# Phase ends without GpSimd's drain, and three reorderings in the middle phase of a macaron block

## The chip, the cores and the metric

The kernel runs on one core of a Trainium2 chip. Its engines are PE (TensorE, matmuls), ACT (ScalarE), DVE (VectorE), POOL (GpSimd, which here also issues the indirect DMAs) and SP (SyncE, which issues the plain DMAs). The metric is the device time in microseconds, the median of several runs; smaller is better.

## The reference

The input is x of 4 x 2048 tokens, 256 wide (8192 rows). Three layers are added to it in turn, each on the layer-normed rows:

```
x = x + 0.5 * ffn(layernorm(x))      # mixture of 8 experts, each token goes to 2
x = x + attn(layernorm(x))           # causal linear attention, 16 heads of 16
x = x + 0.5 * ffn(layernorm(x))      # the same experts again
```

The ffn multiplies each row by Wr (256 x 8), takes the two largest logits and their softmax, and gives each token a position in its two experts' lists in token order; an expert keeps at most 2560 tokens and drops the rest. An expert computes (silu(t W1) * (t W3)) W2 with 1024 hidden columns, and the weighted results of a token are added up. The attention has no softmax: Y of a token is its Q times the running sum of K V' over the tokens before it and itself, then a 16 x 16 product per head made of Ltri, then Wc.

## The kernel before

There are four phases, and each is one `nc.Block()`: a stretch in which each engine runs its own list of instructions, and at whose end all engines meet at a barrier.

- **Route** (`route_phase`, Block at L710) norms the rows, writes them to memory as `normed_rows`, makes the logits, and builds `slot_token`, the table that says which token stands in which slot of which expert. At its end VectorE reads the table and makes the counts of tiles, and GpSimd gathers the rows of the first tile into `xrow` (`Ahead.gather`, four indirect DMAs, one of 128 rows each).
- **Experts** (`expert_phase`, L1038, run twice) goes through the eight experts, each in tiles of 3 or 4 times 128 tokens. Float32 products are made of three matmuls of high and low parts (L100 to L102). GpSimd gathers the rows of the next tile (L438) and scatters the results of the tile before with an adding indirect DMA (L1061) into the rows `x` or `out`. SP loads each expert's weights, 12 pieces of 256 KB, into `raw`; its first act in the phase is such a load (L639).
- **Middle** (`middle_phase`, L1370) goes through 64 chunks of 128 tokens, in 8 groups of 8. A step n of its loop projects q, k and v of chunk n + 2, makes the scores of n + 1 and the result of n. Routing for the second ffn is spread over the steps of the next group: with c the step's number in the group, the moments of the new rows come at c = 0, the choice of experts at c = 1, ScalarE's Exp of the weights at c = 2 (`Router.weigh`, L270), the places at c = 3, and VectorE's `pick_cols` (L345) at c = 5 and 6, whose products PE adds up at c = 7 (`tabulate`, L358). GpSimd makes `pick_rows` (L334).

`x1`, the rows that the middle phase reads, lie in `raw`, which the expert phase uses for weights. What the first expert phase has scattered must have landed before x1 is read. The wait for this stood at the head of the middle phase: GpSimd waits for `y_added`, counts up `all_added`, and SP then issues the four small loads of group 0 (L451) and the large ones of groups 1 and 2 (L1374). PE's first work is to turn chunk 0 (L1412), ScalarE copies it (L1525), PE projects (L1421, L1427), and ScalarE writes the values scaled by the squared inverse deviation `rsq` (L1545, `keep_v`), which VectorE makes with all moments of the group at once (`moments_x1`, L1627).

Two waits of the steps matter. PE turns the keys (L1478) once ScalarE has copied keys, values and three forms of q (L1530 to L1537), and those copies stood behind the Exp in the step c = 2. VectorE adds the result of a chunk (L1616, L1618, `add_out`) when PE has made it (L1484), and `pick_cols` stood behind it.

Of the kernel before, what the change touches and what calls it, by code (L numbers as in the profile page):

```python
# [137 lines left out]
class Norm:  # L138
# [15 lines left out]
    def deviation(self, dve, n):  # L154
        dve.drain()
        for c in range(n):
            dve.bn_aggr(self.mv[:, c, :], self.stats[:, c, :])
        dve.drain()
        dve.tensor_scalar(self.var[:, 0:n], self.mv[:, 0:n, 1], EPS, None, ALU.add)
        dve.drain()  # L160
        inverse_root(dve, self.rstd[:, 0:n], self.seed[:, 0:n], self.var[:, 0:n])
# [262 lines left out]
class Ahead:  # L424
# [3 lines left out]
    def __init__(self, m):  # L428
        self.xrow = m.sb("xrow", [P, BIG, DX])
        self.rows_loaded = [m.sem(f"rows_loaded{i}") for i in range(2)]  # L430
        self.y_added = [m.sem(f"y_added{i}") for i in range(2)]
        self.all_added = m.sem("all_added")
        self.x_first = [m.sem(f"x1_first{i}") for i in range(MG // 2)]
        self.x_loaded = [m.sem(f"x1_loaded{b}") for b in range(3)]
# [6 lines left out]

    def hold_results(self, m):
        self.yrow = m.sb("yrow", [P, BIG, D])

    def wait_added(self, pool, k, n, phase):

        wait_alone(pool, self.y_added[phase], 16 * BIG * n + 16 * SMALL, k.passed)
# [203 lines left out]
def route_phase(nc, k, attention, x_in, xn_out, x1_out, out, slot_token, w, slot_a, raw, raw_loaded, ahead,  # L651
# [4 lines left out]
    with ExitStack() as ctx:  # L656
# [53 lines left out]
        with nc.Block() as block:  # L710
# [162 lines left out]
            @block.gpsimd  # L873
            def _(pool):
                su.make_masks(pool)
                pool.wait_ge(su.marks, 1)
                for g in range(GR - 1):
                    for i in quads(g):
                        r.pick_rows(pool, g, g % 2, quad(g, i), i)
                    if g >= 1:  # L880
                        for q in range(2 * g - 2, 2 * g):
                            pool.wait_ge(w_high, q + 1)
                            pool.tensor_tensor(piece(slot_a[:, 1], q), piece(raw, q), piece(slot_a[:, 0], q).bitcast(F32),
                                               ALU.subtract).then_inc(w_low, 1)
                pool.wait_ge(cleared, 16 * 3)
                for i in range(RING):
                    pool.wait_ge(xn_stored[i], 16 * (BLOCKS // RING))
                pool.wait_ge(r.slots_ready, 1)
                ahead.gather(pool, xn_out, slot_token, 0)

# [79 lines left out]
def expert_phase(nc, k, name, phase, xn, acc, slot_token, w, slot_a, raw, raw_loaded, ahead, table, loaded):  # L970
# [5 lines left out]
    with ExitStack() as ctx:  # L976
# [16 lines left out]
        yrow, y_added = ahead.yrow, ahead.y_added[phase]  # L993
# [19 lines left out]
        y_kept = m.sem("y_kept")  # L1013
        w_high = m.sem("w_high")
# [23 lines left out]
        with nc.Block() as block:  # L1038
            @block.sync
            def _(sp):  # L1040
                load_expert(sp, w, 1, raw, raw_loaded)
                with sp.Fori(0, E - 2) as e:
                    sp.wait_ge(w_low, PIECES * (e + 2))
                    load_expert(sp, w, e + 2, raw, raw_loaded)
                sp.wait_ge(w_low, PIECES * E)
                load_expert(sp, w, 0, raw, raw_loaded)
                wait_raw(sp, raw_loaded, loaded + E - 2)

            @block.gpsimd
            def _(pool):  # L1050
# [86 lines left out]
                if phase == 1:  # L1137
                    ahead.wait_added(pool, k, n, phase)
# [3 lines left out]
            def _(pe):  # L1142
# [59 lines left out]
                turn(16 * SMALL, SMALL)  # L1202
# [92 lines left out]
def middle_phase(nc, k, x1_in, xn_out, x2_out, slot_token, raw, ahead, tiles_in, tiles_out):  # L1295
# [5 lines left out]
    with ExitStack() as ctx:  # L1301
# [68 lines left out]
        with nc.Block() as block:  # L1370
            @block.sync
            def _(sp):
# [3 lines left out]
                sp.wait_ge(ahead.all_added, 1)  # L1376
                ahead.load_x1(sp, x1, x1_g)
# [15 lines left out]
            def _(pool):  # L1393
                ahead.wait_added(pool, k, pool.value_load(tiles_in.first[0:1, E:E + 1], min_val=3 * E, max_val=E * MAX_TILES), 0)
                pool.nop().then_inc(ahead.all_added, 1)
# [126 lines left out]
            def _(act):  # L1522
# [16 lines left out]
                def keep_v(n):  # L1539
                    g, c = divmod(n, MG)  # L1540
                    act.wait_ge(v_made, n + 1)
                    if c == 0:
                        act.wait_ge(n1_ready, g + 1)
# [24 lines left out]
                for n in STEPS:  # L1568
                    g, c = divmod(n, MG)
                    if c == 2 and g >= 1:  # L1570
                        r.weigh(act, g - 1, MG)
# [14 lines left out]
                    if 1 <= c <= 4 and g >= 1:  # L1586
                        norm_x2(g - 1, 2 * c - 2)
                        norm_x2(g - 1, 2 * c - 1)

            @block.vector  # L1590
            def _(dve):
# [33 lines left out]
                def moments_x1(g):  # L1625
                    norm1[g % 2].deviation(dve, MG)
                    dve.tensor_tensor(rsq[:, g % 2, :], norm1[g % 2].rstd[:], norm1[g % 2].rstd[:],  # L1627
                                      ALU.mult).then_inc(n1_ready, 1)
# [12 lines left out]
                for c in range(MG):  # L1641
                    stats_x1(0, c)
                moments_x1(0)
                for n in STEPS:
# [10 lines left out]
                    if chunk(n):  # L1655
                        keep_state(n)
                    if chunk(n):
                        add_out(n)
                        stats_x2(n)
# [7 lines left out]
                    if c in (5, 6) and g >= 1:  # L1667
# [43 lines left out]
def macaron(nc, x, wqT, wkT, wvT, wcT, wc, ltriT, wr, w1, w3, w2, out):  # L1711
# [3 lines left out]
    with ExitStack() as ctx:  # L1715
# [10 lines left out]
        ahead.hold_results(m)  # L1726
        expert_phase(nc, k, "e1_", 0, xn, x1, slot_token, weights, slot_a, raw, raw_loaded, ahead, tiles[0], 2)
        middle_phase(nc, k, x1, xn, out, slot_token, raw, ahead, tiles[0], tiles[1])
# [26 lines left out]
```

## Time and profile before

| | us |
|---|---|
| median of 3 runs | 2999.72 (2999.57 to 2999.74) |
| profiled execution | 3000.1 |
| its span, first to last instruction | 2998.4 |
| PE busy | 2840.5 (95%) |
| VectorE busy | 1617.6 (54%) |
| ScalarE busy | 1274.0 (42%) |
| GpSimd busy | 1167.4 (39%) |

The page of the profile gives busy times as shares of the whole span, and a chain of work that ended last. In such a kernel, with phases of different kinds, they say that PE is nearly always busy but not where it is not. That is read from windows cut at the phases' ends, from the waits of one engine in one stretch, and from timelines of a few microseconds. The engines' queues have records of their own (POOLq, DVEq and so on): the DRAIN with which an engine comes to a barrier, and the semaphore instructions of the barrier. Both carry the line of the Block.

### The profile page before, as it was taken

How to read it: one execution, taken by the hardware profiler on the slowest of the kernel's cores; microseconds unless marked ns; L12 is line 12 of the kernel's file. 1: busy time of each engine (PE TensorE's matmuls, PEld its weight loads, DVE VectorE, ACT ScalarE, POOL GpSimd, SP SyncE). 2: the span in 40 equal slices, each digit the busy share in tenths (PEclk: the TensorE clock that was granted, in tenths of full speed). 3: DMA queues.
4: the chain of work that ended last, by engine and by line, in shares of the span. 5: the costliest groups of instructions: out<-in, count | busy, mean ns of one | idle time of the engine just before them, and what ended most of it. 6: DMA issues, size and time to landing. Idle time of an engine off the chain costs nothing. (4 is left out here: it accounts for less than half of the span.)

```text
span 2998.4 us, 54774 instructions
## 1 busy us (share of the span) xinstructions
PE 2840.5 (95%) x18723; PEld 2543.4 (85%) x18723; DVE 1617.6 (54%) x3791; ACT 1274.0 (42%) x2685; POOL 1167.4 (39%) x1550
## 2 busy tenths in 40 slices
PE   4399999999999999979999995999999999999998
PEld 3389899989999989868888884998999998899987
DVE  8844445455454545447877876445545454545443
ACT  5244444444344434334444443344434343444443
POOL 3754444444444434310211122443444543444433
PEclk8699999999999999989999997999999999999999
DMA  7542323232332322120112013322323231323212
GB/s 248 183 126 34 84 35 81 41 78 39 83 70 48 83 36 36 36 55 30 59 50 67 30 44 94 85 43 71 86 36 78 43 84 30 81 41 78 43 34 29
DMA packets 155114, 197.23 MB, mean 66 GB/s; under 512 B 15536, under 2 KB 127024, under 8 KB 154928
## 3 DMA queue, kind: packets, MB, share of 16 engines
q0 software_dynamic: 62688, 87.11, 17.2%
q1 hardware_dynamic: 81952, 97.30, 9.9%
q10 hardware_dynamic: 10288, 10.38, 1.0%
q8 instruction: 112, 1.84, 0.2%
q14 instruction: 74, 0.61, 0.1%
HBM read 124.32 MB, written 78.79 MB: 68 GB/s over the span
## 5 line engine op out<-in xcount | busy, mean ns | idle before, releaser
L1267 DVE TENSOR_TENSOR e_h_lo<-e_hid,e_h_hi 128x384 fp32r<-128x384 f32 (+1 forms) x640 | 384.4, 601 | 399.0 <-ACT e_h_hi L1228 391.6
L1264 DVE TENSOR_TENSOR e_hid<-e_ps,e_gate 128x384 f32<-128x384 f32 (+1 forms) x640 | 381.5, 596 | 373.4 <-ACT e_gate L1224 364.0
L1228 ACT ACTIVATE e_h_hi<-e_hid 128x384 fp32r<-128x384 f32 (+1 forms) x640 | 356.8, 558 | 422.6 <-DVE e_hid L1264 417.5
L1224 ACT ACTIVATE e_gate<-e_ps 128x384 f32<-128x384 f32 (+1 forms) x640 | 333.8, 522 | 407.9 <-PE e_ps L102 399.9
L100 PE MATMUL e_ps<-e_xT_hi,e_wb 128*128 128x384 f32 (+1 forms) x1280 | 456.5, 357 | 0.0
L101 PE MATMUL e_ps<-e_xT_lo,e_wb 128*128 128x384 f32 (+1 forms) x1280 | 455.0, 355 | 0.0
L102 PE MATMUL e_ps<-e_xT_hi,e_wb 128*128 128x384 f32 (+1 forms) x1280 | 454.9, 355 | 0.0
L100 PE MATMUL e_ps<-e_xT_hi,c_wa 128*128 128x384 f32 (+1 forms) x1280 | 451.2, 353 | 2.5 <-DVE e_xT_lo L1256 2.5
L102 PE MATMUL e_ps<-e_xT_hi,c_wa 128*128 128x384 f32 (+1 forms) x1280 | 449.4, 351 | 0.0
L101 PE MATMUL e_ps<-e_xT_lo,c_wa 128*128 128x384 f32 (+1 forms) x1280 | 449.2, 351 | 0.0
L438 POOL DMA_INDIRECT c_xrow<-normed_rows,e_token x320 | 346.6, 1083 | 155.7 <-issue 83.8
L1061 POOL DMA_INDIRECT out<-c_yrow,e_y_token x163 | 272.8, 1673 | 124.5 <-DVE c_yrow L1277 79.8
L1061 POOL DMA_INDIRECT x<-c_yrow,e_y_token x163 | 272.1, 1669 | 123.8 <-DVE c_yrow L1277 75.3
L100 PEld LDWEIGHTS e_ps<-e_xT_hi,e_wb 128*128 128x128 f32 x1280 | 240.5, 188 | 22.3 <-DVE e_hid L1264 1.6
L100 PEld LDWEIGHTS e_ps<-e_xT_hi,c_wa 128*128 128x128 f32 x1280 | 242.1, 189 | 20.0 <-issue 3.3
L102 PEld LDWEIGHTS e_ps<-e_xT_hi,e_wb 128*128 128x128 f32 x1280 | 240.6, 188 | 18.9
L101 PEld LDWEIGHTS e_ps<-e_xT_lo,e_wb 128*128 128x128 f32 x1280 | 240.6, 188 | 18.4
L102 PEld LDWEIGHTS e_ps<-e_xT_hi,c_wa 128*128 128x128 f32 x1280 | 241.9, 189 | 14.1
L101 PEld LDWEIGHTS e_ps<-e_xT_lo,c_wa 128*128 128x128 f32 x1280 | 242.2, 189 | 13.4
L1164 PE MATMUL e_psy<-c_wa,e_h_hi 128*128 128x512 f32 x640 | 234.5, 403 | 0.0
L1164 PE MATMUL e_psy<-e_wb,e_h_hi 128*128 128x512 f32 x640 | 230.6, 396 | 0.0
L334 POOL TENSOR_SCALAR mi_r_picked_row<-c_steps,mi_r_rowf 128x128 f16<-128x128 f16 x112 | 64.9, 598 | 422.1 <-DVE mi_r_colf L318 422.1
(297 smaller groups left out, 4767.3 us busy)
## 6 DMA issues: line engine op xcount, KB each, us to landing
c_raw<-w SPq DMA_DIRECT2D x204, 256.0 KB
normed_rows<-r_xn SPq DMA_DIRECT2D x8, 1056.0 KB, 7.0
normed_rows<-mi_xn SPq DMA_DIRECT2D x8, 1056.0 KB, 4.7
x<-x ACTq DMA_DIRECT2D x8, 1024.0 KB, 12.3
out<-mi_x SPq DMA_DIRECT2D x8, 1024.0 KB, 5.3
r_xin<-x SPq DMA_DIRECT2D x7, 1024.0 KB, 10.9
c_raw<-x SPq DMA_DIRECT2D x7, 1024.0 KB, 8.5
c_xrow<-normed_rows,e_token POOLq DMA_INDIRECT x320
```

The lines of the kernel that those rows point to most:

```text
L100: pe.matmul(out, a[0], b[0], start=first, stop=False)
L101: pe.matmul(out, a[0], b[1], start=False, stop=False)
L102: return pe.matmul(out, a[1], b[0], start=False, stop=last)
L334: ins = eng.tensor_scalar(self.picked_row[:, self.ring_at(q) + c, j, :], self.k.steps[:, 0:P], self.rowf[b][:, i * QUAD + c, j:j + 1], Non ...
L438: pool.indirect_dma_start(self.xrow[:, sub, :], None, xn, bass.IndirectOffsetOnAxis(ap=token[:, sub:sub + 1], axis=0), bounds_check=ROWS - ...
L1061: pool.indirect_dma_start(acc, bass.IndirectOffsetOnAxis(ap=y_token[:, sub:sub + 1], axis=0), yrow[:, sub, :], None, bounds_check=ROWS - 1 ...
L1164: pe.matmul(bank[:].rearrange("p (u d) -> p u d", u=2), h[0][:, f, own], both[:, :, at:at + D], start=(f == 0), stop=False)
L1224: act.activation(gate[:, f % 2, 0:n], ps1[f % 2][:, 0:n], ACT.Silu).then_inc(gated, 1)
L1228: act.activation(h[0][:, f, 0:n], hid[:, f % 2, 0:n], ACT.Copy).then_inc(h_high, 1)
L1264: dve.tensor_tensor(hid[:, f % 2, 0:n], ps3[f % 2][:, 0:n], gate[:, f % 2, 0:n], ALU.mult).then_inc(hid_ready, 1)
L1267: dve.tensor_tensor(h[1][:, f, 0:n], hid[:, f % 2, 0:n], h[0][:, f, 0:n].bitcast(F32), ALU.subtract).then_inc(h_ready, 1)
```

## The change

1. The Blocks of route, experts (both runs) and middle are opened with `no_gpsimd_drain=True`: GpSimd comes to the barrier without a DRAIN of its engine. Three waits are added for what the drain had covered: in route GpSimd waits for the low parts of the first weights (`w_low`); in the expert phase it waits in both runs for its scatters (`y_added`), counts up `all_added`, and then comes to the barrier; PE's first turn in an expert phase waits for all four gathers instead of three quarters of their count.
2. The first four x1 loads are issued by SP at the end of the first expert phase, behind `all_added`, instead of at the head of the middle phase.
3. In the middle phase ScalarE's Exp moves from the head of the step c = 2 to its end.
4. For the last group of steps `pick_cols` of group 6 stands in front of `add_out` of the same step instead of behind it.
5. The moments of group 0 are made for chunks 0 and 1 by themselves, then for the other six; ScalarE waits accordingly.

```
@@ Norm
-    def deviation(self, dve, n):
+    def deviation(self, dve, n, lo=0):
         dve.drain()
-        for c in range(n):
+        for c in range(lo, n):
             dve.bn_aggr(self.mv[:, c, :], self.stats[:, c, :])
...                                   # var, rstd, seed likewise [:, lo:n]
@@ route_phase, expert_phase, middle_phase
-        with nc.Block() as block:
+        with nc.Block(no_gpsimd_drain=True) as block:
@@ route_phase, gpsimd
                 ahead.gather(pool, xn_out, slot_token, 0)
+                pool.wait_ge(w_low, PIECES)
@@ expert_phase, sync
                 wait_raw(sp, raw_loaded, loaded + E - 2)
+                if phase == 0:
+                    sp.wait_ge(w_low, PIECES * (E + 1))
+                    sp.wait_ge(all_added, 1)
+                    ahead.load_x1(sp, rows_of(raw), groups_of(acc))
@@ expert_phase, gpsimd
-                if phase == 1:
-                    ahead.wait_added(pool, k, n, phase)
+                wait_alone(pool, y_added, WORDS * n + 16 * SMALL, k.passed)
+                pool.nop().then_inc(all_added, 1)
                 wait_alone(pool, x_loaded, WORDS * n + WORDS, k.passed)
@@ expert_phase, tensor
-                turn(16 * SMALL, SMALL)
+                turn(WORDS, SMALL)
@@ middle_phase, sync
-                sp.wait_ge(ahead.all_added, 1)
-                ahead.load_x1(sp, x1, x1_g)
                 load(1)
@@ middle_phase, gpsimd
-                ahead.wait_added(pool, k, pool.value_load(tiles_in.first[0:1, E:E + 1], ...), 0)
-                pool.nop().then_inc(ahead.all_added, 1)
@@ middle_phase, scalar, keep_v
-                    if c == 0:
-                        act.wait_ge(n1_ready, g + 1)
+                    if n == 0:
+                        act.wait_ge(n1_ready, 1)
+                    if n == 2 or c == 0 and g >= 1:
+                        act.wait_ge(n1_ready, g + 2)
@@ middle_phase, scalar, the loop over steps
-                    if c == 2 and g >= 1:
-                        r.weigh(act, g - 1, MG)
...
                         norm_x2(g - 1, 2 * c - 1)
+                    if c == 2 and g >= 1:
+                        r.weigh(act, g - 1, MG)
@@ middle_phase, vector
-                for c in range(MG):
+                for c in range(2):
                     stats_x1(0, c)
-                moments_x1(0)
+                moments_x1(0, 0, 2)
+                for c in range(2, MG):
+                    stats_x1(0, c)
+                moments_x1(0, 2, MG)
...
+                    last = g == MGS - 1
+                    if c in (5, 6) and last:
+                        r.pick_cols(dve, g - 1, (g - 1) % 2, MQ * (g - 1) + c - 5, c - 5)
                     if chunk(n):
                         add_out(n)
                         stats_x2(n)
...
-                    if c in (5, 6) and g >= 1:
+                    if c in (5, 6) and g >= 1 and not last:
                         r.pick_cols(dve, g - 1, (g - 1) % 2, MQ * (g - 1) + c - 5, c - 5)
```

## Rows read from the trace of the kernel before

**Rows 1.** Windows by stage: us, busy us of each engine, granted clock, DMA share, GB/s.
```profile
153.20:1296.90 1143.70, 1142.11 (x6278) 1043.52 (x6278) 547.41 (x949) 494.67 (x950) 504.32 (x642) 1.00 0.29 60
...
1326.60:1807.00 480.40, 470.67 (x5426) 391.85 (x5425) 366.74 (x1202) 213.84 (x629) 64.90 (x112) 1.00 0.14 44
```

**Rows 2.** Barrier of the route phase, by line: duration ns min/median/max, first and last start.
```profile
L710 POOLq DRAIN  x1: 6164/6164/6164, 146.8 to 146.8; - x1
L710 DVEq DRAIN  x1: 165/165/165, 151.6 to 151.6; - x1
```

**Rows 3.** The same for the two expert phases.
```profile
L1038 POOLq DRAIN  x2: 4882/6387/7892, 1298.8 to 2993.3; - x2
```

**Rows 4.** The same for the middle phase.
```profile
L1370 POOLq DRAIN  x1: 5802/5802/5802, 1837.5 to 1837.5; - x1
L1370 DVEq DRAIN  x1: 165/165/165, 1838.5 to 1838.5; - x1
```

**Rows 5.** Timeline, route to experts: start us, us, engine, line, idle before and releaser.
```profile
149.94 1.01 POOL L438 DMA_INDIRECT c_xrow<-normed_rows,c_slot_token  x1 [0.30 <-issue]
...
153.53 0.87 PE L1150 MATMUL e_psx<-c_ident,c_xrow 128*128 128x128 f32 x3 [10.63 <-PEq L710]
```

**Rows 6.** Timeline, experts to middle.
```profile
1298.87 1.55 POOL L1061 DMA_INDIRECT x<-c_yrow,e_y_token  x1 [1.21 <-DVE c_yrow L1277]
...
1307.69 1.90 SPq L451 DMA_DIRECT2D c_raw<-x  x4
...
1310.50 0.69 PE L1412 MATMUL mi_xv<-c_ident,c_raw 128*128 128x128 f32 x2 [13.56 <-DMA c_raw<-x]
...
1319.63 0.47 ACT L1545 ACTIVATE mi_vpad<-mi_xv,mi_rsq 128x256 f32<-128x256 f32 x1 [2.70 <-DVE mi_rsq L1627]
```

**Rows 7.** Windows of 1 us in the middle phase; the clock is the third column from the right.
```profile
1317.00:1318.00 1.00, 0.42 (x2) 0.18 (x2) 0.67 (x4) 0.00 (x0) 0.00 (x0) 1.00 1.06 336
...
1320.00:1321.00 1.00, 0.69 (x2) 0.29 (x2) 0.00 (x0) 0.49 (x4) 0.00 (x0) 0.50 0.00 0
...
1809.00:1810.00 1.00, 1.00 (x9) 0.78 (x12) 0.32 (x1) 0.00 (x0) 0.00 (x0) 0.50 0.00 0
```

**Rows 8.** Timeline, PE's projections of chunks 1 and 2.
```profile
1321.38 3.78 PE L1421 MATMUL mi_qk<-mi_xT,c_wqk 128*128 128x128 f32 x16 [0.47 <-ACT mi_xT L1525]
...
1329.48 2.05 PE L1421 MATMUL mi_qk<-mi_xT,c_wqk 128*128 128x128 f32 x16 [0.53 <-ACT mi_xT L1525]
```

**Rows 9.** Waits of PE from 1328 to 1807: us in total, times, longest.
```profile
PE mi_qk L1478 <- ACT mi_qT L1537: 6.3, 8, 1.1
```

**Rows 10.** Timeline of PE in the third step of a group.
```profile
1408.20 0.71 PE L1471 MATMUL mi_kv<-mi_vpad,mi_krow 128*128 128x128 f32 x4
1409.72 0.44 PE L1478 MATMUL mi_qk<-c_ident,mi_kT 128*128 128x128 f32 x2 [0.80 <-ACT mi_qT L1537]
```

**Rows 11.** Timeline, last steps of the middle phase.
```profile
1799.18 0.23 DVE L1616 SCALAR_TENSOR_TENSOR mi_lgs<-mi_yo,mi_n_rstd,mi_lgx 128x8 f32<-128x8 f32 x1 [0.56 <-PE mi_yo L1484]
...
1804.76 0.20 DVE L1616 SCALAR_TENSOR_TENSOR mi_lgs<-mi_yo,mi_n_rstd,mi_lgx 128x8 f32<-128x8 f32 x1
...
1805.73 1.92 DVE L345 TENSOR_SCALAR mi_r_picked_col<-c_steps,mi_r_colf,c_code 128x160 f16<-128x160 f16 x8
...
1807.80 1.23 PE L358 MATMUL mi_xv<-mi_r_picked_col,mi_r_picked_row 128*128 128x160 f16 x8 [3.71 <-DVE mi_r_picked_col L345]
```

**Rows 12.** Timeline, middle to experts.
```profile
1840.27 1.01 POOL L438 DMA_INDIRECT c_xrow<-normed_rows,c_slot_token  x1 [0.30 <-issue]
...
1843.91 0.88 PE L1150 MATMUL e_psx<-c_ident,c_xrow 128*128 128x128 f32 x3 [10.21 <-PEq L1370]
```

**Rows 13.** Timeline of POOL in the second expert phase.
```profile
1882.95 0.63 POOL L1081 COPY e_next_weight<-c_xrow 128x4 f32<-128x4 f32 x1 [5.86 <-DMA c_xrow<-normed_rows,e_token]
...
1906.92 0.19 POOL L1081 COPY e_next_weight<-c_xrow 128x4 f32<-128x4 f32 x1 [1.96 <-DMA c_xrow<-normed_rows,e_token]
...
2989.45 1.54 POOL L1061 DMA_INDIRECT out<-c_yrow,e_y_token  x1 [1.21 <-DVE c_yrow L1277]
```

More of the change, by code:

```diff
@@ L152, in statistics @@
         dve.bn_stats(self.stats[:, c, :], src)
-    def deviation(self, dve, n):
+    def deviation(self, dve, n, lo=0):
         dve.drain()
-        for c in range(n):
+        for c in range(lo, n):
             dve.bn_aggr(self.mv[:, c, :], self.stats[:, c, :])
         dve.drain()
-        dve.tensor_scalar(self.var[:, 0:n], self.mv[:, 0:n, 1], EPS, None, ALU.add)
+        dve.tensor_scalar(self.var[:, lo:n], self.mv[:, lo:n, 1], EPS, None, ALU.add)
         dve.drain()
-        inverse_root(dve, self.rstd[:, 0:n], self.seed[:, 0:n], self.var[:, 0:n])
+        inverse_root(dve, self.rstd[:, lo:n], self.seed[:, lo:n], self.var[:, lo:n])
     def moments(self, dve, done, n):
@@ L430, in __init__ @@
         self.rows_loaded = [m.sem(f"rows_loaded{i}") for i in range(2)]
-        self.y_added = [m.sem(f"y_added{i}") for i in range(2)]
-        self.all_added = m.sem("all_added")
         self.x_first = [m.sem(f"x1_first{i}") for i in range(MG // 2)]
@@ L440, in gather @@
                 bounds_check=ROWS - 1, oob_is_err=True).then_inc(self.rows_loaded[phase], 16)
[L442 to L447, printed above, removed]
     def load_x1(self, sp, x1, x1_g):
@@ L992, in expert_phase @@
         h = [m.sb("h_hi", [P, KF, WIDE], F32R), m.sb("h_lo", [P, KF, WIDE], F32R)]
-        yrow, y_added = ahead.yrow, ahead.y_added[phase]
+        yrow = m.sb("yrow", [P, BIG, D])
         ps1 = [m.ps(f"ps1_{b}") for b in range(2)]
@@ L1013, in expert_phase @@
         y_kept = m.sem("y_kept")
+        y_added = m.sem("y_added")
+        all_added = m.sem("all_added")
         w_high = m.sem("w_high")
@@ L1036, in total @@
             return eng.value_load(table.first[0:1, E:E + 1], min_val=3 * E, max_val=E * MAX_TILES)
-        with nc.Block() as block:
+        with nc.Block(no_gpsimd_drain=True) as block:
             @block.sync
@@ L1292, in groups_of, with middle_phase @@
     return t[0:T, :].rearrange("(g c p) d -> g p c d", p=P, c=MG)
-def middle_phase(nc, k, x1_in, xn_out, x2_out, slot_token, raw, ahead, tiles_in, tiles_out):
+def middle_phase(nc, k, x1_in, xn_out, x2_out, slot_token, raw, ahead, tiles_out):
     with ExitStack() as ctx:
@@ L1368, in states @@
             return (CB - 1) * (n // CB) + n % CB
-        with nc.Block() as block:
+        with nc.Block(no_gpsimd_drain=True) as block:
             @block.sync
@@ L1393, in _ @@
             def _(pool):
-                ahead.wait_added(pool, k, pool.value_load(tiles_in.first[0:1, E:E + 1], min_val=3 * E, max_val=E * MAX_TILES), 0)
-                pool.nop().then_inc(ahead.all_added, 1)
                 for b in range(3):
@@ L1623, in stats_x1, with moments_x1 @@
                     norm1[g % 2].statistics(dve, x1[:, g % 3, c, :], c)
-                def moments_x1(g):
-                    norm1[g % 2].deviation(dve, MG)
-                    dve.tensor_tensor(rsq[:, g % 2, :], norm1[g % 2].rstd[:], norm1[g % 2].rstd[:],
+                def moments_x1(g, lo=0, hi=MG):
+                    norm1[g % 2].deviation(dve, hi, lo)
+                    dve.tensor_tensor(rsq[:, g % 2, lo:hi], norm1[g % 2].rstd[:, lo:hi], norm1[g % 2].rstd[:, lo:hi],
                                       ALU.mult).then_inc(n1_ready, 1)
@@ L1725, in macaron @@
         route_phase(nc, k, attention, x, xn, x1, out, slot_token, weights, slot_a, raw, raw_loaded, ahead, tiles[0])
-        ahead.hold_results(m)
         expert_phase(nc, k, "e1_", 0, xn, x1, slot_token, weights, slot_a, raw, raw_loaded, ahead, tiles[0], 2)
-        middle_phase(nc, k, x1, xn, out, slot_token, raw, ahead, tiles[0], tiles[1])
+        middle_phase(nc, k, x1, xn, out, slot_token, raw, ahead, tiles[1])
         expert_phase(nc, k, "e2_", 1, xn, out, slot_token, weights, slot_a, raw, raw_loaded, ahead, tiles[1], 2 + E)
```

## The prediction

> **What bounds the kernel now.** I read the windows by stage first. In the first expert phase PE is busy 1142.11 of 1143.70 us at a granted clock of 1.00, in the middle phase 470.67 of 480.40 us [rows 1]; the second expert phase reads like the first. The change touches no instruction of the expert tiles, so what it can win lies at the seams between the four phases and in the 9.7 us that PE idles in the middle. For the seams I read the barrier's own instructions by line (L710, L1038, L1370), then the timeline around each seam; for the middle the waits of PE. In the rows of the barriers the reader sees GpSimd's DRAIN at 6164, 7892 (the first expert phase) and 5802 ns, and 4882 ns at the program's end, where the rows for VectorE say 165 [rows 2 to 4].
>
> **The change part by part.** Times are those of the profiled execution: span 2998.4, whole run 3000.1 us.
>
> *Route to experts.* The drain holds the barrier to 146.8 + 6.16 = 153.0, and PE begins 153.53 [rows 2, 5]. Without it the last to arrive is VectorE, 151.6 + 0.17 = 151.8; with the same 0.55 from barrier to PE that is 152.3. But the first turn now waits for all four gathers (WORDS in place of 48). The fourth issue ends 149.94 + 1.01 = 150.95 [rows 5]; in the loop a gather is seen 1.96 us after its last issue [rows 13], which gives 152.9. So PE gains between 0.6 and 1.2; I take 0.8, nearer the gather. The wait on w_low that GpSimd gets costs nothing: VectorE makes those pieces before the tile table on which it arrives at 151.8 anyway, and nothing stands behind it on GpSimd's queue but the barrier.
>
> *Experts to middle.* GpSimd's last scatter issue ends 1298.87 + 1.55 = 1300.42, the drain at 1306.7, SP issues the first x1 load at 1307.69, PE turns it at 1310.50, 2.81 later [rows 3, 6]. Now GpSimd waits for the scatters before the barrier: in phase two, which does this already, its queue comes through 2.3 us after the last issue (2989.45 + 1.54 = 2990.99, drain from 2993.3) [rows 3, 13]. So all_added at 1302.7, SP issues at once, behind a w_low wait long fulfilled, and PE turns at 1305.6: 4.9 earlier. SP itself now arrives at the barrier only after four issues, 1.90 us [rows 6], at 1304.7; the others start the middle at about 1305.0, still ahead of the landing. GpSimd's three memsets, for which ScalarE waits, then end about 1306.5, 0.1 late for it. Net 4.8. The next loads of 1 MB stay behind the four small ones, as before.
>
> *Two chunks' moments.* ScalarE idles 2.70 us before chunk 0's values, for the moments of all eight chunks [rows 6]. It is free at 1316.93, 6.4 us after PE's turn; the moments came 9.1 us after it, with three more quarters of x1 to land and eight aggregations in that time. Two chunks need neither. Bounds 0 and 2.7; I take 2.7. The other six are due only at chunk 2, and the second pass of some 13 small instructions lies in VectorE's wait for the first scores.
>
> *Clock in that stretch.* The granted clock is 1.00 in 1317 to 1318 and 0.50 in 1320 to 1321 [rows 7]: PE had little to do from 1318 to 1320, which is the wait just removed. Chunk 1's 16 projections run 3.78 us there, chunk 2's 2.05 [rows 8]. If the clock stays up, that is 1.73, and some 0.7 by the same ratio for the value projection behind: 2.4. Bounds 0 and 2.4; I take 2.4, since the clock was already up before the gap. The seam and its start give 4.8 + 2.7 + 2.4 = 9.9.
>
> *The power at a step's end.* PE waits 6.3 us in 8 places for the q copies of ScalarE [rows 9]. About 0.6 of it is the first chunk's; seven waits are in the third step of a group, where ScalarE stands before the Exp for VectorE's choice. Start to start, PE takes 1.52 us from update to turn, 0.71 of it busy and 0.80 idle [rows 10]; since weight loads overlap in the dense steps, I put the loss at 0.17 more than the idle. Seven groups: 5.7 + 7 x 0.17 = 6.9, bounds 5.7 and 7.0; I take 6.8. What is moved is one small ACTIVATE (and once its table load) into ScalarE's wait ahead of the next keys; VectorE asks for its result only in the next step. Next late is nothing: PE fills.
>
> *Group 6's columns.* Near the end PE idles 3.71 us for the second pick_cols. That pick starts at 1805.73, behind an add_out begun at 1804.76; put first it starts 0.97 earlier. The first pick now fills the 0.56 us for which VectorE waited on project_out [rows 11]. Together 1.53. The price is a result that is added 1.9 us later at step 61; PE's next state product waits for it, but there PE has slack, being due back only at the pick. Afterwards the clock is at 0.50 [rows 7]; with PE's gap down from 3.71 to 2.2 us or less it may stay up, worth up to 1.6, and I take 1.2. Sum 2.7, bounds 1.5 and 3.1.
>
> *Middle to experts.* VectorE arrives 1838.5 + 0.17; without the drain (1837.5 + 5.80 = 1843.3) the barrier opens some 4.6 us earlier [rows 4]. PE can't use it: it waits for the fourth gather, issued until 1840.27 + 1.01 = 1841.28 [rows 12], and SP's burst of twelve weight loads, the first thing SP does in the phase, now starts near 1839.0 on top of it. A gather is seen 1.96 us after its issue, or 5.86 where it runs beside such a burst [rows 13]: PE begins at 1843.2 or 1847.1 against 1843.91. Half the burst's lead is missing here, so I take the middle, 3.9 us, 1845.2: a loss of 1.3. Bounds -0.7 and +3.2.
>
> The Trainium skill (DMA: Bandwidth & Descriptors, section Queues, rings and completion order) says that each DMA engine takes turns between its queues packet by packet. By that a burst could delay the gather by no more than about its own length; this trace does not agree, 5.86 stands against 1.96. By the rule the sum would be 2.0 us lower (a rival below).
>
> *End.* The last drain runs 4882 ns from 2993.3, to the end of the span [rows 3]. With the same block's end undrained 4.9 goes; if what ends the run waits for GpSimd all the same, 0. I take 4.9, because the scatters had landed before that drain began, so nothing that must be waited for is left.
>
> On drains the Trainium skill (VectorE: DVE Perf Modes, section The DRAIN you can't avoid) speaks against this change: DRAINs of the frame around a kernel are a constant 12 ns or so on all five engines. The trace agrees for SP and not for GpSimd. By that rule the 0.8, 4.8 and 4.9 are no gain and the 1.3 no loss, and the sum is -14.6 in place of -23.8; the rival of the moved drain below ends at the same time.
>
> Sum: -0.8 - 9.9 - 6.8 - 2.7 + 1.3 - 4.9 = -23.8, thus 3000.1 - 23.8 = 2976.3 for an execution like the profiled one. The median of the runs is 0.4 lower (2999.72): 2976.
>
> **The rivals.**
> - *Turns between queues* (0.12): the gather of the third seam isn't delayed and PE starts it at 1843.2. 2974.
> - *The end's drain is waited for anyway* (0.13), by whatever closes the run outside the span. For: 1.7 us lie between span and run, unexplained. Against: the scatters are in. 2976 + 4.9 = 2981.
> - *The clock doesn't follow* (0.08): it falls in the gaps that remain. For: it fell after some 2 us without PE work. 2.4 + 1.2 lost: 2979.5.
> - *The drain moves instead of going* (0.05): GpSimd has the same work to do before its next instruction, so that the memsets and SP's wait start no earlier. 0.8, 4.8 and 4.9 are lost, the 1.3 saved: 2985. Against: between a scatter and the next copy in the loop there are about 2 us, not 5.
> - *Slower* (0.02): the clock falls in the expert phases, since PE goes into them with shorter rests. 2287 us run at 1.00 [rows 1]; 0.99 for their mean costs 23 us and cancels everything, 0.98 gives 3022. Against: 1142 us of unbroken PE work didn't lower it.
> - *No change* (0.02): several of these together.
>
> **How the numbers follow.** The forecast itself has 0.58: 2976. The unknown terms reach from 2973 to 2990 if all fall one way; with the rivals, 2972 to 2985 leaves out about 2 in 10. A measurement here tells 0.2% (6 us, 2993.7) from no change. All but the last two cases end below it: faster 0.96, same 0.02, slower 0.02.
>
> **What would show it.** Right: no DRAIN of GpSimd at the ends of the blocks; PE's first turn at 152.3 to 152.9; from the last scatter issue of the first expert phase to SP's first x1 load 2.3 us in place of 7.3; ScalarE no longer waits for moments at chunk 0; clock 1.00 for chunk 1's projections; the 6.3 us of PE behind ScalarE down to under 1; span end about 2.4 us after the last scatter issue. Wrong: gathers at the third seam seen after 1.96 or after 5.86; a tail between last record and run longer than 1.7; a PE wait that moves from q copies to prob or x2.

## The result, and the profile after

| | before | after |
|---|---|---|
| median of the runs, us | 2999.73 (2999.57 to 3000.72, 4 runs) | 2976.41 (2975.67 to 2978.79, 4 runs) |
| ratio, 95% interval | 1 | 0.9923 [0.9906, 0.9940] |
| profiled execution: run, span, us | 3000.1, 2998.4 | 2975.74, 2974.0 |
| mean granted clock of the span | 0.973 | 0.978 |

23.3 us less by the medians, 24.4 by the two profiled executions; forecast was 2976 (23.8 less). In a second measurement, beside runs of before, the changed kernel gave 2977.79 against 2999.71 (e9 below). One of the six executions of e4 below ran in a slower state (3222.08 us at a mean granted clock of 0.835), and the median given for e4 is that of the other five.

The two dense stretches are nearly what they were [rows 1]: windows by stage of the kernel after (length in us; busy us of PE, PE's weight loads, VectorE, ScalarE, GpSimd; granted clock, DMA share, GB/s).

```profile
152.70:1295.10 1142.40, 1140.99 (x6278) 1042.24 (x6278) 547.41 (x949) 495.93 (x950) 503.56 (x642) 1.00 0.30 60
1314.70:1787.00 472.30, 469.21 (x5426) 391.65 (x5426) 366.22 (x1203) 216.31 (x629) 65.17 (x112) 1.00 0.14 44
```

In the middle PE does 469.21 us of work in a stretch of 472.30; before it was 470.67 in 480.40. Its idle time has gone from 9.7 to 3.1 us.

Barriers of the blocks after, by line (duration in ns min/median/max, first and last start). L701, L1032 and L1368 are before's L710, L1038 and L1370. No line has a DRAIN of GpSimd, which [rows 2 to 4] have at 4.9 to 7.9 us:

```profile
L701 DVEq DRAIN  x1: 181/181/181, 151.6 to 151.6; - x1
L1032 SPq DRAIN  x2: 7/65/123, 1302.9 to 2711.3; - x2
L1368 DVEq DRAIN  x1: 210/210/210, 1817.0 to 1817.0; - x1
```

The timeline after, for [rows 5, 6, 8, 11 and 12] (start us, us, engine, line, operation, idle before and releaser). Lines are up to 9 lower than before's, and `c_yrow` is called `e_yrow`.

```profile
149.95 1.01 POOL L436 DMA_INDIRECT c_xrow<-normed_rows,c_slot_token  x1 [0.30 <-issue]
152.77 1.54 PE L1148 MATMUL e_psx<-c_ident,c_xrow 128*128 128x128 f32 x6 [9.87 <-DMA c_xrow<-normed_rows,c_slot_token]
...
1296.96 1.55 POOL L1059 DMA_INDIRECT x<-e_yrow,e_y_token  x1 [1.21 <-DVE e_yrow L1275]
1300.90 1.90 SPq L442 DMA_DIRECT2D c_raw<-x  x4
1303.77 0.69 PE L1406 MATMUL mi_xv<-c_ident,c_raw 128*128 128x128 f32 x2 [8.75 <-DMA c_raw<-x]
1304.76 0.39 ACT L1519 ACTIVATE mi_xT<-mi_xv 128x256 f32<-128x256 f32 x1 [9.17 <-POOL mi_vpad L1391]
1310.28 0.49 ACT L1541 ACTIVATE mi_vpad<-mi_xv,mi_rsq 128x256 f32<-128x256 f32 x1
1311.81 2.05 PE L1415 MATMUL mi_qk<-mi_xT,c_wqk 128*128 128x128 f32 x16 [0.47 <-ACT mi_xT L1519]
...
1781.91 0.71 PE L1439 MATMUL mi_yo<-mi_qT,mi_state 128*128 128x128 f32 x4 [0.84 <-DVE mi_x L1614]
1787.03 0.71 PE L358 MATMUL mi_xv<-mi_r_picked_col,mi_r_picked_row 128*128 128x160 f16 x8 [1.18 <-DVE mi_r_picked_col L345]
...
1817.49 6.35 SPq L630 DMA_DIRECT2D c_raw<-w  x12
1818.28 1.02 POOL L436 DMA_INDIRECT c_xrow<-normed_rows,c_slot_token  x1 [0.30 <-issue]
1823.73 1.54 PE L1148 MATMUL e_psx<-c_ident,c_xrow 128*128 128x128 f32 x6 [12.01 <-DMA c_xrow<-normed_rows,c_slot_token]
...
2969.80 1.54 POOL L1059 DMA_INDIRECT out<-e_yrow,e_y_token  x1 [1.20 <-DVE e_yrow L1275]
```

What the reader is to see: PE's first turn of the experts (the transposes of the rows just gathered) is released by the gather, no longer by the barrier; SP issues the x1 loads 2.4 us after GpSimd's last issue ended (1298.51) in place of 7.3; ScalarE's values of chunk 0 (1310.28) wait for nothing; chunk 1's projections take 2.05 us where they took 3.78; at 1823.73 it is again the gather that releases PE, 4.43 us after its issue ended (1819.30), with SP's twelve loads beside it; and the span ends 2.7 us behind the end of the last scatter issue (2971.34). The run ends 1.7 us behind the span, before and after.

Windows of 1 us after, for [rows 7]; the clock is the third column from the right.

```profile
157.00:158.00 1.00, 1.00 (x5) 1.00 (x5) 0.00 (x0) 1.00 (x1) 0.84 (x7) 0.50 0.67 236
159.00:160.00 1.00, 1.00 (x7) 1.00 (x7) 0.09 (x1) 0.62 (x2) 0.93 (x1) 1.00 0.97 348
1312.00:1313.00 1.00, 1.00 (x10) 1.00 (x10) 0.71 (x5) 0.00 (x0) 0.00 (x0) 1.00 0.30 95
1789.00:1790.00 1.00, 0.50 (x12) 0.26 (x2) 0.00 (x0) 0.39 (x1) 0.00 (x0) 1.00 0.00 0
```

Waits of PE from 1316 to 1783 (us in total, times, longest), for [rows 9]: the q copies, 6.3 us in 8 places, are down to the first chunk's. The wait for `mi_x` (x2) is new.

```profile
PE mi_yo L1439 <- DVE mi_x L1614: 0.8, 1, 0.8
PE mi_qk L1472 <- ACT mi_qT L1531: 0.6, 1, 0.6
```

### The profile page after: what moved, and what is told of

It is laid out like the page before. It is cut to its first block, busy times and chain, and to the rows that moved or that the text cites. A ratio compares the mean times of both kernels' runs of the same rounds, so it can differ in the third digit from the quotient of the medians.

```text
span 2974.0 us, 54813 instructions
## 1 busy us (share of the span) xinstructions
PE 2836.9 (95%) x18723; PEld 2539.4 (85%) x18723; DVE 1620.2 (54%) x3804; ACT 1278.8 (43%) x2685; POOL 1168.3 (39%) x1550
## 4 chain that ended last, share of the span: by engine, by line
PE 54%; DVE 1%; issue 0%; ACT 0%; DMA 0%; POOL 0%; DVEq 0%; POOLq 0%; ACTq 0%
PE e_ps L100 8%; PE e_ps L101 8%; PE e_ps L102 8%; PE e_psy L1162 5%; PE mi_qk L1415 4%; PE e_ps L1162 3%; PE e_psy L1164 3%; PE mi_sc L1431 2%; PE mi_yo L1451 2%; PE mi_xv L1421 2%; PE mi_yo L1478 2%; PE e_ps L1164 2%; PE mi_kv L1465 1%; PE e_psx L1148 1%; PE mi_yo L1439 1%; PE mi_qk L1472 0%
## 5 line engine op out<-in xcount | busy, mean ns | idle before, releaser
L1059 POOL DMA_INDIRECT out<-e_yrow,e_y_token x163 | 274.1, 1682 | 126.6 <-DVE e_yrow L1275 71.3
L1059 POOL DMA_INDIRECT x<-e_yrow,e_y_token x163 | 273.9, 1680 | 125.7 <-DVE e_yrow L1275 76.1
```

Source lines behind the costliest of these rows:

```text
L1059: pool.indirect_dma_start(acc, bass.IndirectOffsetOnAxis(ap=y_token[:, sub:sub + 1], axis=0), yrow[:, sub, :], None, bounds_check=ROWS - 1 ...
```

## The experiments

All are edits of the kernel after, four to six executions each, in four groups (e1 to e4, e5 to e8, e9 to e11, e12), each group beside its own runs of before (medians 2999.12, 2998.27, 2999.71, 3000.44). The column "less" is that median minus the kernel's. The parts are those of the one profiled execution of each. The route phase, which only e1, e10, e11 and e12 touch, began the experts anywhere from 151.65 to 155.81 us, so the parts of a span tell more than its sum. **A** is from PE's first turn of the first experts to its first turn of the middle, **M** from there to the end of the fourth gather's issue, **lag** from there to PE's first turn of the second experts, **D** from there to the end of the span.

| profiled | median of runs | less | A | M | lag | D |
|---|---|---|---|---|---|---|
| before | 2999.73 | | 1156.97 | 530.78 | 2.63 | 1154.50 |
| after | 2976.41 | 23.3 | 1151.00 | 515.53 | 4.43 | 1150.32 |
| e9, after again | 2977.79 | 21.9 | 1150.80 | 515.27 | 5.38 | 1150.04 |
| e1, all drains back | 2982.57 | 16.6 | 1153.63 | 516.17 | 2.68 | 1155.03 |
| e2, moments at once | 2980.32 | 18.8 | 1151.44 | 519.47 | 4.92 | 1149.35 |
| e3, Exp at the head | 2985.48 | 13.6 | 1151.69 | 522.89 | 5.36 | 1150.47 |
| e4, columns behind | 2981.45 | 17.7 | 1150.99 | 519.82 | 5.72 | 1150.82 |
| e5, last drain back | 2984.27 | 14.0 | 1151.92 | 515.72 | 5.58 | 1155.36 |
| e6, middle's drain back | 2978.64 | 19.6 | 1151.48 | 515.55 | 6.88 | 1149.72 |
| e7, burst held | 2974.84 | 23.4 | 1151.74 | 516.10 | 1.90 | 1150.69 |
| e8, second pick alone | 2980.02 | 18.2 | 1151.56 | 517.88 | 5.25 | 1152.02 |
| e10, kept busy | 2977.91 | 21.8 | 1151.17 | 515.98 | 5.21 | 1151.48 |
| e11, e10 and burst held | 2975.03 | 24.7 | 1151.79 | 516.01 | 1.91 | 1150.42 |
| e12, hardly a rest | 2969.38 | 31.1 | 1149.20 | 515.45 | 2.16 | 1147.62 |

Where no edit touches it, A is 1150.8 to 1151.9, M 515.3 to 516.1 and D 1149.4 to 1152.0, so a part tells about 1 us. Inside M the steps repeat far better: from the first scores of the middle to the state product of step 62 (1314.68 to 1781.91 in after) it is 467.20 to 467.23 us in the ten executions that no edit touches there. The scatter of M lies ahead of it, 10.7 to 11.5 us from PE's turn to those scores.

**e1_drains_back**

```
-        with nc.Block(no_gpsimd_drain=True) as block:    (route, experts, middle)
+        with nc.Block() as block:
```

> The changed kernel with GpSimd's drain back at the end of all four blocks, everything else kept. Theory (the drains cost what stood behind them): route to experts +0.8 (barrier at 146.8 + 6.2 = 153.0 in place of 152.0); experts to middle +3.0, not +4.9, because SP issues the x1 loads before the barrier now and only GpSimd's memsets and ScalarE's first copy come late; middle to experts -1.9 (the gathers land before the weight burst begins); end +4.9. Sum +6.8: 2983.2. Rival (the drains only stood where GpSimd waited anyway, or move): no difference, 2976.4. Rival (the third seam's loss is not the missing drain): +8.7, 2985.

Barriers of e1 by line:

```profile
L701 POOLq DRAIN  x1: 4737/4737/4737, 150.2 to 150.2; - x1
L701 DVEq DRAIN  x1: 165/165/165, 153.6 to 153.6; - x1
L1032 POOLq DRAIN  x2: 4882/4884/4887, 1304.0 to 2977.9; - x2
L1368 POOLq DRAIN  x1: 5864/5864/5864, 1821.5 to 1821.5; - x1
```

PE turned 1.9 us after VectorE's arrival at the first barrier (155.50 against 153.6), in place of 1.17: +0.7. A is 2.7 longer (expected 3.0), D 4.9 longer, and the lag is back to 2.68. The sum, 0.7 + 2.7 + 4.9 - 2.7 = 5.6 against e9's lag, lies between the medians' 4.8 and 6.2 (2982.57 against 2977.79 and 2976.41; M, 0.6 to 0.9 longer, is not in it). So the drains do cost what stands behind them, and with them back the loss at the third seam is gone. The rival of no difference falls, and so does that of a third seam that stays late (2985, lag unchanged).

**e5_end_drain**

```
-        with nc.Block(no_gpsimd_drain=True) as block:    (expert_phase)
+        with nc.Block(no_gpsimd_drain=phase == 0) as block:
```

> The changed kernel with GpSimd's drain back at the last block alone. Theory: the run ends 4.9 us later, 2981.3, and the span with it. Rival (whatever closes the run outside the span waits for GpSimd anyway): the span grows and the run does not, 2976.4.

Barrier of e5's last block:

```profile
L1032 POOLq DRAIN  x1: 5222/5222/5222, 2978.9 to 2978.9; - x1
```

D is 5.0 to 5.3 longer (4.9 expected), and the run follows the span (2986.08 against 2984.4 in the profiled one, 1.7 as ever). Nothing outside the span waits for GpSimd all the same: that rival falls. The medians show more than the edit's part, 6.5 (against e9) to 7.9 (against after), where 2981.3 was expected. In the profiled execution PE began the experts at 155.81, 1.2 and 3.0 us later than there, which no edit of e5 touches; whether that is the rest in the other executions too, no run shows.

**e6_middle_drain**

```
-        with nc.Block(no_gpsimd_drain=True) as block:    (middle_phase)
+        with nc.Block() as block:
```

> The changed kernel with GpSimd's drain back at the end of the middle alone. Theory (the weight burst starting 2 us before the fourth gather's issue delays it): the drain ends about 2.0 us after that issue, the burst begins behind it, PE turns near 1821.9 in place of 1823.7: -1.8, 2974.6. Rival (the gather is late for a reason of its own): the barrier and the gather's 4.4 us both stand in the way, 0 to +0.6.

Barrier and timeline of e6:

```profile
L1368 POOLq DRAIN  x1: 10072/10072/10072, 1817.8 to 1817.8; - x1
```
```profile
1820.54 1.02 POOL L436 DMA_INDIRECT c_xrow<-normed_rows,c_slot_token  x1 [0.30 <-issue]
...
1828.44 1.51 PE L1148 MATMUL e_psx<-c_ident,c_xrow 128*128 128x128 f32 x6 [14.45 <-PEq L1368]
```

A miss for both theories. The drain ended 6.3 us after the last gather issue (1827.9 against 1821.56), where in before and e1 it ended 2.0 after it (1843.3 against 1841.28, 1827.36 against 1825.30), so PE came later, not earlier. The code at this place is e1's; what differs is that no earlier block has drained. That alone doesn't make a drain long: e5's, also the first at the end of a block, took 5.22 us. Why it is 10.07 here in place of 5.86 us is left open. On the gather e6 says nothing; e7 does.

**e7_burst_late**

```
             def _(sp):
+                if phase == 1:
+                    sp.wait_ge(x_loaded, WORDS)
                 load_expert(sp, w, 1, raw, raw_loaded)
```

> The changed kernel; SP's first weight load of the second expert phase waits for the four gathers. Theory (burst against gather): the gather is seen 1.9 to 2.0 us after its last issue, PE turns at 1821.3 in place of 1823.7: -2.4, 2974.0, less what the later weights cost, at most 1. Rival (turns between queues, the gather needs 4.4 us by itself here): PE stays at 1823.7 and the weights come 4 us later, 0 to +2.

Timelines of e7, and of e9 (the kernel after) for comparison. The gather row is the fourth, and its issue ends at start plus length:

```profile
1820.81 1.02 POOL L436 DMA_INDIRECT c_xrow<-normed_rows,c_slot_token  x1 [0.31 <-issue]
...
1823.73 1.54 PE L1150 MATMUL e_psx<-c_ident,c_xrow 128*128 128x128 f32 x6 [9.48 <-DMA c_xrow<-normed_rows,c_slot_token]
```
```profile
1819.63 1.02 POOL L436 DMA_INDIRECT c_xrow<-normed_rows,c_slot_token  x1 [0.30 <-issue]
...
1826.03 1.33 PE L1148 MATMUL e_psx<-c_ident,c_xrow 128*128 128x128 f32 x5 [12.96 <-DMA c_xrow<-normed_rows,c_slot_token]
```

Without the burst the gather is there 1.90 us after its issue (1.91 in e11), near the 1.96 of [rows 13]. In the eight executions where the burst began 1.8 us before the issue ended, it took 4.43, 4.92, 5.21, 5.25, 5.36, 5.38, 5.58 and 5.72. The burst costs it some 3.4 us, and held back it costs PE nothing measurable: D is 1150.69. Of the 3.4 us the medians show 1.6 (against the first measurement of after) to 3.0 (against e9). By the column "less", each against its own runs of before, it is 0.1 to 1.5; e11 against e10, in one group, gives 2.9. The intervals of the ratios, 0.9918 [0.9904, 0.9931] and 0.9923 [0.9906, 0.9940] or 0.9930 [0.9917, 0.9944], overlap, so it is the lag that is shown and not the total.

**e2_one_moments**

```
-                for c in range(2):
-                    stats_x1(0, c)
-                moments_x1(0, 0, 2)
-                for c in range(2, MG):
+                for c in range(MG):
                     stats_x1(0, c)
-                moments_x1(0, 2, MG)
+                moments_x1(0)
```

> The changed kernel with the moments of all eight chunks of group 0 at once. Theory: ScalarE waits some 2.7 us for them at chunk 0's values, the granted clock falls to 0.50 in that gap, and chunk 1's projections run 3.8 us in place of 2.05: +2.7 + 2.5 = +5.2, 2981.6. Rival (the clock stays up, since PE came to this place through a shorter seam): +2.7 alone, 2979.1. Rival (the statistics were not what ended the wait): 0.

Timeline of e2, one of its windows, and VectorE's row for the last quarter of x1 before:

```profile
1304.15 0.69 PE L1406 MATMUL mi_xv<-c_ident,c_raw 128*128 128x128 f32 x2 [9.08 <-DMA c_raw<-x]
...
1306.26 1.43 DVE L152 BATCH_NORM_STATS2 mi_n_stats<-c_raw 128x6 f32<-128x256 f32 x4 [0.69 <-DMA c_raw<-x]
...
1312.06 0.47 ACT L1539 ACTIVATE mi_vpad<-mi_xv,mi_rsq 128x256 f32<-128x256 f32 x1 [1.48 <-DVE mi_rsq L1621]
...
1313.81 3.78 PE L1415 MATMUL mi_qk<-mi_xT,c_wqk 128*128 128x128 f32 x16 [0.47 <-ACT mi_xT L1519]
```
```profile
1313.00:1314.00 1.00, 0.53 (x3) 0.19 (x2) 0.00 (x0) 0.38 (x1) 0.00 (x0) 0.50 0.09 17
```
```profile
1314.50 0.75 DVE L152 BATCH_NORM_STATS2 mi_n_stats<-c_raw 128x6 f32<-128x256 f32 x2 [1.21 <-DMA c_raw<-x]
```

From PE's turn to the scores of chunk 0 it takes 15.13 us in place of 10.91: 4.2, of 5.2 expected. The clock does fall in the gap and chunk 1's projections take 3.78 us: 2.8 of the 4.2. The wait itself is worth 1.4 now, not 2.7. The statistics of x1's last quarter, the last of group 0, end at 1307.69 here, 3.5 us behind PE's turn (1304.15). Before they ended at 1315.25, 4.8 behind it (1310.50), and VectorE had waited 1.21 us for that quarter's landing. So 1.2 us of what looked like the moments' cost was a later landing of the last quarter, and went with the seam. What brought it in earlier is not shown: before, SP's two loads of 1 MB followed the quarters at once (1309.64), now the barrier stands between them (1303.40), but no run changes that alone.

**e3_exp_head**

```
                     g, c = divmod(n, MG)
+                    if c == 2 and g >= 1:
+                        r.weigh(act, g - 1, MG)
                     if chunk(n + 2):
...
-                    if c == 2 and g >= 1:
-                        r.weigh(act, g - 1, MG)
```

> The changed kernel with ScalarE's Exp back at the head of the third step of a group. Theory: seven groups lose some 1.0 us each by the wait of the q copies for VectorE's choice: +7.2, 2983.6. Rival (only the idle time of the q waits counts, 0.8 in seven places): +5.7, 2982.1. Rival (part of the gain belonged to the shorter wait of VectorE for positions): under +5.

Waits of PE in e3, from 1316 to 1783:

```profile
PE mi_qk L1472 <- ACT mi_qT L1531: 5.9, 8, 1.1
```

M is 7.4 to 7.6 longer, but 0.5 to 0.7 of that lies ahead of the first scores (11.43 us from PE's turn, 10.91 in after and 10.71 in e9), where the edit doesn't reach. From the first scores to the state product of step 62 it is 474.1 in place of 467.2 us: 6.9, for 5.3 us of idle time more (5.9 - 0.6). What PE loses beyond its idle rows is about 0.2 us a group; that it is the start and end of a pipeline that ran dense is my explanation, and no run tests it. The rival of the idle time alone (it put that at 5.7, and 5.3 is measured) falls, and so does that of under 5. The medians show 7.7 to 9.1 more.

**e4_cols_behind** and **e8_second_front**

```
e4:
-                    last = g == MGS - 1
-                    if c in (5, 6) and last:
-                        r.pick_cols(dve, g - 1, (g - 1) % 2, MQ * (g - 1) + c - 5, c - 5)
...
-                    if c in (5, 6) and g >= 1 and not last:
+                    if c in (5, 6) and g >= 1:
e8:
-                    last = g == MGS - 1
-                    if c in (5, 6) and last:
+                    last = g == MGS - 1 and c == 6
+                    if last:
```

> The changed kernel with both column picks of group 6 behind the result. Theory: PE idles about 3.7 us before the second tabulate product and the clock falls behind it: +1.0 to +1.5 for the gap and +1.2 to +1.6 for the clock, +3.1 in all, 2979.5. Rival (the clock stays up without the change): +1.5, 2977.9.

> The changed kernel with only the second column pick of group 6 in front of the result. Theory A: the first pick in front costs PE 0.84 us at step 61 (its wait for x2) and buys nothing that the second does not buy: -0.8, 2975.6. Theory B (my sum): the first pick fills VectorE's wait of 0.56 us, and without it the chain to the second tabulate is 0.56 later: -0.3 to +0.6.

The second tabulate product and the state product ahead of it in e4, and a window of PE behind them (us, busy, clock, DMA share, GB/s); then the same of e8:

```profile
1780.52 0.71 PE L1439 MATMUL mi_yo<-mi_qT,mi_state 128*128 128x128 f32 x4
...
1788.17 1.23 PE L358 MATMUL mi_xv<-mi_r_picked_col,mi_r_picked_row 128*128 128x160 f16 x8 [3.71 <-DVE mi_r_picked_col L345]
```
```profile
1789.00:1790.00 1.00, 1.00 (x7) 0.50 0.00 0
```
```profile
1782.58 0.71 PE L1439 MATMUL mi_yo<-mi_qT,mi_state 128*128 128x128 f32 x4
...
1789.25 1.23 PE L358 MATMUL mi_xv<-mi_r_picked_col,mi_r_picked_row 128*128 128x160 f16 x8 [2.74 <-DVE mi_r_picked_col L345]
```
```profile
1790.00:1791.00 1.00, 1.00 (x8) 0.50 0.00 0
```

From the state product of step 62 to that tabulate product: 7.65 us in e4, 6.67 in e8, 5.12 after. The second pick in front is worth 0.98 and the first 1.55, less the 0.84 that PE waits for x2 at 1781.91; neither e4 nor e8 has that wait. With gaps of 3.71 and 2.74 us the clock is at 0.50 behind them; with 1.18 it isn't. M is 4.4 longer in e4 (3.1 expected, 1.5 by the rival of a clock that stays up) and 2.5 in e8. So both theories of e8 fall: A put it at -0.8 and B, my sum, at -0.3 to +0.6, and neither had the clock in it, which is 1.6 of the 2.5 (from the second tabulate product to the last result product 4.3 us in place of 2.7). The first pick has its price, but it is what closes the gap far enough for the clock.

**e9_after_again**

> The changed kernel itself once more, as the measure for the kernels beside it and for how far one kernel's seams vary between executions. Expected: 2976.4, 0.9923 of before. If the time from SP's weight burst to the fourth gather's landing is a matter of chance, the third seam (last result product to the second expert phase's first turn, 33.99 us in the first profile) lies between 34 and 36 here.

2977.79 (2977.10 to 2981.26), ratio 0.9930 [0.9917, 0.9944]. Lag 5.38 against 4.43, and last result product to second experts 34.91 against 33.99: the seam lies in the 34 to 36 that were expected, and the first profile of after had the shortest lag of the eight.

**e10_kept_busy**, **e11_busy_late** and **e12_no_rests**

```
+def keep_busy(pe, k, bank, n):
+    for i in range(n):
+        pe.transpose(bank[:, 0:P], k.ident[:], k.ident[:])

 end of route's PE      +  keep_busy(pe, k, turn_banks[0], 36)                      e12: 70
 expert phase, start    +  keep_busy(pe, k, ps1[0], 16 if phase == 1 else 2)        e12: 28, 2
 behind turn(..., SMALL)                                                            e12: 6
 expert phase 0, end    +  keep_busy(pe, k, ps1[0], 50)                             e12: 76
 end of middle's PE     +  pe.wait_ge(kr_kept, NCH)
                        +  keep_busy(pe, k, qk, 21)                                 e12: 34
 (e11, e12: SP's burst held as in e7)
```

> The changed kernel; in the rests before each phase PE transposes the identity into a free bank (36 times before the first experts, 50 before the middle, 21 + 16 before the second experts), so that it does not come out of the rest at a granted clock of 0.50. Theory (each phase begins with 5 to 8 us at half speed, and how long is what differs between executions): about 2.9 us won in the first experts, 2.6 in the middle, 3.7 in the second experts: -9.2, 2967. Rival (the clock does not follow these transposes, or they run past the release): 0 to +1.

> The kernel before this one, with the second phase's weight burst held until the four gathers have landed. Theory (both gains are independent, 2.6 for the gather): -2.6 against it, 2964.5. Rival (the gather's delay is then hidden, or the late weights hold PE up once it runs at full clock from the start): 0 to +1 against it.

> As e11_busy_late, with enough idle transposes that hardly a rest is left: 70 before the first experts, 76 before the middle, 34 + 28 before the second experts, and six behind the first turn of either expert phase. In e11 the clock was back at 1.00 in each rest and fell again 0.2 to 3.8 us after the transposes had stopped for 1.5 to 4.8 us. Theory (those stops are why it fell): the clock stays up through the phases' starts; 3 to 4 us won in each expert phase and 2.6 in the middle: 2966 to 2968. Rival (a start at full clock falls back all the same, since the phases' own first 3 us hold little work for PE): the low stretch stays near 7 us and only moves, 2974 to 2976. Rival (the transposes run past the release): later turns, up to +3.

In e10 the idle transposes ended 3.7, 3.1 and 3.8 us before PE's next instruction, and the clock, 1.00 in part of each rest, was down again near it: it fell 0.8 us behind the first turn, 0.1 ahead of the second and 5.9 ahead of the third. In e11 they ended 4.8, 3.2 and 1.5 us before, and the clock fell between 1.6 us ahead of the turn and 1.2 behind it. Windows of PE in e10, and in e11 (same columns as for e4):

```profile
153.00:154.00 1.00, 0.00 (x0) 1.00 0.38 101
156.00:157.00 1.00, 0.00 (x0) 0.50 0.97 320
```
```profile
1825.00:1827.00 2.00, 0.87 (x6) 0.90 0.32 104
1829.00:1831.00 2.00, 2.00 (x8) 0.50 0.81 249
```

Neither gained by them: e10 is e9 (2977.91, 2977.79), e11 is e7 (2975.03, 2974.84), so e10's theory of -9.2 falls and with it e11's 2964.5. e11's 2.9 us under e10 (2.6 expected) are the held burst once more. In e12 the rests were filled to about 1 us or less. Windows of PE around the two expert starts and the middle's, and PE's last idle transposes ahead of the middle, with its first work there:

```profile
157.00:159.00 2.00, 1.03 (x6) 1.00 0.94 301
...
1308.00:1310.00 2.00, 2.00 (x9) 0.50 0.96 315
...
1824.00:1826.00 2.00, 1.51 (x9) 1.00 0.90 313
```
```profile
1295.80 8.46 PE L614 MATMUL e_ps<-c_ident 128*128 128x128 f32 x76
1304.67 0.41 PE L1418 MATMUL mi_xv<-c_ident,c_raw 128*128 128x128 f32 x2 [0.41 <-PEq L1038]
1306.55 2.90 PE L1427 MATMUL mi_qk<-mi_xT,c_wqk 128*128 128x128 f32 x16 [1.47 <-ACT mi_xT L1533]
```

The theory's half on the expert phases holds, its half on the middle does not. Both expert phases begin at 1.00: A is 1.6 to 2.5 and D 2.4 to 3.1 shorter than in e7 and e9, where 3 to 4 each were expected. In the middle PE waited 1.47 us for ScalarE behind its first turn, the clock fell at 1307.55, and nothing was won: 10.90 us from turn to scores, 10.91 in after. e12 differs from e11 in two ways, by longer filling ahead of the turns and by six transposes behind the first turn of either expert phase; no run has one without the other. The lag is 2.16 and not 1.90, since the filling ahead of the last turn ended only at 1822.22. The run is 2969.38 (2968.08 to 2971.59), 0.9895 [0.9879, 0.9912] of before: 31 us less. Its interval lies below that of e9 and overlaps that of e7, [0.9904, 0.9931]. It is the fastest of the versions.

## Why the prediction held, point by point

The total, 2976 against 2976.41, rests on every sign being right and on errors of up to 1.2 us that cancelled; that it came within 0.5 us is luck. By the parts:

- **Route to experts, -0.8.** -0.76 in the profiles (153.53 to 152.77), with VectorE reaching the barrier at 151.6 in both; +0.7 when the drain came back. Held, and the gather was the next to be late, as said.
- **Clock in the first expert phase: no term.** From PE's first turn to the last scatter issue it took 1145.34 us before [rows 5, 6] and 1144.19 after. The clock rose 8.8 us behind the first turn then and 5.9 now. This 1.15 was no part of the forecast. The clock's rise behind a rest differs from execution to execution; in e12, where the phase begins at 1.00, A is 1.6 to 2.5 shorter.
- **Experts to middle, -4.8.** From last scatter issue to PE's turn: 11.63 to 6.81, -4.8. GpSimd's memsets end ScalarE's wait (1304.76), 0.2 late for 0.1 said. Held; with the drain back e1 gives 2.7 of it up and not 4.8. The other 2.1 I put down to SP's issue, which is ahead of the barrier now; no run moves that back alone.
- **Two chunks' moments, -2.7, and clock, -2.4.** Turn to values of chunk 0: 9.13 to 6.51, -2.6; values to scores: 6.96 to 4.40, -2.6. Both terms held in size, but the first was ascribed wrongly by half: e2 gives 1.4 for the edit, the other 1.2 came with the earlier landing of x1's last quarter.
- **Power at a step's end, -6.8.** -7.2 between the profiles, 6.9 by e3, around the upper bound of 7.0. Held: the 0.17 that was put on top of a group's idle time is 0.2 by both.
- **Group 6's columns, -2.7.** 2.53 for the earlier pick, less 0.84, and 1.46 for the clock: -3.15, just above the bound of 3.1. The step that failed in it is "there PE has slack": it had none, and waited 0.84 us for x2. A wait for x2 was named as a sign of being wrong; it came from the first pick, not from the moved Exp (e3 still has it, e4 and e8 don't). Against that the first pick brought 1.55 in place of 0.56. Undone (e4) it costs 4.4; the clock stayed low for 6.8 us there and for 3.4 before.
- **Middle to experts, +1.3.** This is the term that was mis-sized most. The burst delays the gather to 5.3 us in the middle of eight executions, where I took 3.9 because "Half the burst's lead is missing here": half the lead did not mean half the delay. The profile of after had the shortest, 4.43, so the seam lost 1.8 there and 2.8 in e9, the bound being 3.2. The rival of turns between queues (gather at 1.96) falls with e7 and e9. The Trainium skill (DMA: Bandwidth & Descriptors, section Queues, rings and completion order) has each DMA engine change queues only after a whole packet. No run here shows how long such a packet lasts, so the runs don't decide on the rule. What they refute is my reading of it, by which the gather would hardly be delayed: 5.3 stands against 1.90.
- **End, -4.9.** Last scatter issue to end of span: 8.95 to 4.2, -4.7; 5.0 to 5.3 by e5's D. Held, the run follows the span.
- **Drains.** The rival that the drain moves gave 2985, and e1 and e5 decide against it: GpSimd's DRAIN at a block's end took 4.7 to 10.1 us, and what stood behind it came earlier without it. My use of the Trainium skill (VectorE: DVE Perf Modes, section The DRAIN you can't avoid) gave 2985 too. That section's 12 ns are for the DRAINs of the frame ahead of and behind a kernel; a block's end is another place, and the figure should not have been carried over to it.
- **Slower by the clock in the expert phases**: 1.00 over 1142.40 us, no trace of it.

## What to carry to other kernels

Before a barrier's drain is dropped, ask what it kept apart: here it held a weight burst back until a small gather had landed, and one wait on the gather's semaphore (e7) gives that back without the drain. Idle time of the matrix engine was worth more than its rows say, by some 0.2 us at each of seven stops of a dense pipeline (e3), and by the clock where it falls behind the gap (it did behind 2.74 and 3.71 us here, and not behind 1.18); such a gap is worth shortening even where it can't be closed. And where a phase starts from rest, filling the rests with idle matrix work up to their last microsecond, with some more behind the first turn, took 5.5 us off this kernel (e12 against e7), while filling that stopped 1.5 to 4.8 us early took off nothing (e10, e11).

## What the hardware showed unasked

- GpSimd's DRAIN at a block's end is no constant: 4.74 to 6.16 us in eight of ten records (5.22 in e5, where it is the only one), 7.89 where it began during the scatters, and 10.07 in e6, where it is the only one too. Not explained.
- The granted clock rose 5.7 to 8.8 us behind PE's first work of an expert phase (e12 aside, which begins at 1.00), differently in each execution (in after 5.9 and 7.5 us, 158.7 against 152.77 and 1831.2 against 1823.73; in e9 5.7 and 6.7). Beside it the start of the experts varies by 4 us. Whether the two make up the scatter between runs is not shown, since each kernel has one profiled execution, and after has two.
